# The recurrence stage of a two-layer kernel: its 512-token batches written out, layernorm two batches ahead, the dots of two heads issued as a pair

## What is computed

```python
xn = _layernorm(x)                       # (8, 512, 256), eps 1e-5
gamma = sigmoid(decay)                   # one per head, 4 heads of 64
v = (xn @ W_write.T) split in 4 heads
rk = xn split in 4 heads;  wk = rk moved one token later, zero first
# scan over chunks of 64 tokens; written without chunks, for token p of a head:
reads[p] = sum over k < p of gamma**(p-1-k) * (rk[p] . wk[k]) * v[k]
s = xn + (exp(log_alpha) * reads) @ W_read.T
```

## Time and profile before

| what | value |
|---|---|
| runs shown (3) | median 3754.51 us, 3751.19 to 3755.1 |
| the profiled execution, own time | 3755.62 us |
| its span, first to last instruction | 3753.9 us |
| granted TensorE clock, mean over the span | 0.947 |
| PE, PEld, DVE, ACT, POOL busy over the span | 91%, 69%, 66%, 58%, 31% |
| first dot and last `finish` of the recurrence | 2252.05 and 2529.12 us |

### The profile page before, as it was taken

How to read it: one execution, slowest core, us unless ns; L and a number is a source line. 1 busy time by engine, 2 the same in 40 slices (tenths; PEclk the granted TensorE clock), 3 DMA queues, 4 the chain that set the end, 5 groups by cost and what they waited for, 6 DMA issues and landing times. The chain is left out here.

```text
span 3753.9 us, 68147 instructions
## 1 busy us (share of the span) xinstructions
PE 3413.5 (91%) x19130; PEld 2589.2 (69%) x19130; DVE 2466.6 (66%) x7055; ACT 2174.9 (58%) x5066; POOL 1178.1 (31%) x1802
## 2 busy tenths in 40 slices
PE   2999999999999999989999978887999976799995
PEld 2777777777777777758888854444666655688885
DVE  5777777777777777776666643335666645466665
ACT  1777777777777777755565541113656551455553
POOL 1333333333333333334333420004131301244342
PEclk9999999999999999999999987887999985899998
DMA  4221222222122122234334420101111113445455
GB/s 160 46 49 43 49 49 45 47 49 48 44 49 49 43 49 49 47 108 141 117 123 138 131 95 23 34 28 41 27 30 28 28 43 135 150 120 141 129 133 151
DMA packets 177637, 282.42 MB, mean 75 GB/s; under 512 B 32499, under 2 KB 119283, under 8 KB 177523
## 3 DMA queue, kind: packets, MB, share of 16 engines
q1 hardware_dynamic: 162930, 261.03, 24.0%
q0 software_dynamic: 14592, 19.93, 3.3%
HBM read 161.89 MB, written 41.16 MB: 54 GB/s over the span
## 5 line engine op out<-in xcount | busy, mean ns | idle before, releaser
L723 POOL TENSOR_SCALAR at_p<-at_p,at_recip 128x128 f32<-128x128 f32 (+3 forms) x1028 | 537.0, 535 | 979.5 <-DVE at_recip L862 979.5
L773 ACT ACTIVATE at_p<-at_p,at_nmax 128x128 f32<-128x128 f32 (+3 forms) x1030 | 575.6, 559 | 290.1 <-DVE at_nmax L856 286.8
L856 DVE CUSTOM_DVE_ANT_0 at_p<-at_s_ps,at_bias 128x128 f32<-128x128 f32 (+3 forms) x1030 | 493.6, 479 | 153.7 <-PE at_s_ps L971 153.7
L978 PE MATMUL at_t_ps<-ident,at_p 128*128 128x128 f32 x2560 | 459.7, 277 | 0.4 <-POOL at_p L723 0.4
L970 PE MATMUL at_s_ps<-at_k_twice,at_q 128*128 128x128 f32 (+3 forms) x1030 | 387.7, 377 | 8.0 <-DVE at_nmax L856 1.2
L1748 DVE CUSTOM_DVE_ANT_0 aa_a_ps<-aa_a_ps,aa_hidden 128x128 f32<-128x128 f32 (+3 forms) x512 | 247.4, 507 | 175.9 <-PE aa_a_ps L1912 172.7
L971 PE MATMUL at_s_ps<-at_k_twice,at_q 128*128 128x128 f32 (+3 forms) x1030 | 332.3, 323 | 0.0
L978 PEld LDWEIGHTS at_t_ps<-ident,at_p 128*128 128x128 f32 x2560 | 294.7, 140 | 46.3 <-DVE at_pT L869 30.0
L988 PE MATMUL at_o_ps<-at_pT,at_v 128*64 128x512 f32 (+3 forms) x2064 | 306.3, 439 | 0.0
L1648 ACT ACTIVATE aa_pT<-aa_b_ps 128x512 f32<-128x512 f32 (+1 forms) x384 | 196.6, 529 | 178.6 <-PE aa_b_ps L1930 175.7
L988 PEld LDWEIGHTS at_o_ps<-at_pT,at_v 128*64 128x64 f32 x2064 | 136.7, 136 | 175.8 <-issue 156.9
(11 more groups left out here) (316 smaller groups left out, 8611.9 us busy)
## 6 DMA issues: line engine op xcount, KB each, us to landing
at_k_twice<-at_k_parts SPq DMA_DIRECT2D x260, 256.0 KB, 3.3
nw_w_raw<-in_w_all_dram SPq DMA_DIRECT2D x52, 1024.0 KB, 7.4
w_raw<-in_w_dram SPq DMA_DIRECT2D x57, 768.0 KB
ln_x<-in_x_dram SPq DMA_DIRECT2D x10, 512.0 KB, 4.7
nw_xh<-xh_dram SPq DMA_DIRECT2D x10, 512.0 KB, 4.3
nw_xl<-xl_dram SPq DMA_DIRECT2D x10, 512.0 KB, 4.9
rc_x<-x_dram SPq DMA_DIRECT2D x10, 512.0 KB, 3.8
at_w_raw<-in_w_heads_dram SPq DMA_DIRECT2D x18, 256.0 KB, 3.4
```

The costliest lines, as they stand in the source:

```text
L723: pool.tensor_scalar(p, p, recip[:, u:u + 1], 1.0, ALU.mult, ALU.mult).then_inc(scaled, 1)
L773: act.activation(p_sb[:, u, 0:N], p_sb[:, u, 0:N], ACT.Exp, bias=nmax[:, u:u + 1], scale=-1.0, accum_out=total[:, u:u + 1]).then_inc(exped, 1)
L856: dve.tensor_tensor_reduce(out=p_sb[:, u, 0:N], in0=s_ps[u % 2][:, 0:N], in1=bias[:, u % 2, S - N:S], scale=1.0, scalar=BIG, op0=ALU.add, ...
L978: ins = pe.transpose(t_ps[u % 2][:, k * P:k * P + P], p_sb[:, u, k * P:k * P + P], ident[:])
```

## The change

Nothing outside `recurrence_phase` changes. Inside:

- The loops over pairs of batches (`Fori`) are written out for all 8 batches; the last two loads of `x_in`, which nobody read, are gone, and so are SP's waits for a finished store.
- `norm` writes `y` directly, without the copy; transposition and squares read `y`. It is cut in three, `weigh_spread`, `sum_spread` and `norm`, and done for batch n+2 while batch n is worked on, between the decays.
- The banks `xT_ps` are gone: `turn` writes its two halves into `n_ps`, which it shares with `values` and `mix`. The freed banks go to `d_ps`, now four: two pairs, of one bank for each of two heads.
- `dots(n, g, t)` issues the products of heads 2g and 2g+1 for the same t one behind the other, in rows 0 to 63 and 64 to 127 of the array and in different banks. `turn`, `reads`, `values` and `mix` are cut in pieces that stand between the pairs. `mix` of batch n comes in batch n+1.
- ACT takes the half-turns one by one, and does `rms` behind them.

```diff
@@ tensor
-            def dots(n, par, h):
-                row = slice(HD * (h % 2), HD * (h % 2) + HD)
-                for i in range(TT):
-                    pe.wait_ge(decayed, n * (RH * TT) + (h * TT + i + 1))
-                    pe.matmul(d_ps[i % 2][:, 0:WIDTHS[i]], yT[par][row, h // 2, P * i:P * i + P],
-                              yT[par][row, h // 2, 1 + P * i:1 + S], start=True, stop=True).then_inc(dotted, 1)
+            def dots(n, g, t):
+                number = pair_no(n, g, t)          # (n * KT + g) * TT + t
+                if number >= 2:
+                    pe.wait_ge(decayed, 2 * number - 2)
+                for h in range(2):
+                    rows = slice(HD * h, HD * h + HD)
+                    pe.matmul(d_ps[t % 2][h][:, 0:WIDTHS[t]], yT[n % 2][rows, g, P * t:P * t + P],
+                              yT[n % 2][rows, g, 1 + P * t:1 + S], start=True, stop=True).then_inc(dotted, 1)
+            def turn(n, k):
+                pe.wait_ge(normed, n * TT + TT)
+                if n == 1:
+                    pe.wait_ge(value_out, k + 1)
+                if n >= 2:
+                    pe.wait_ge(s_done, 2 * (n - 2) + k + 1)
+                for i in range(TT):
+                    ins = pe.transpose(n_ps[k][:, P * i:P * i + P], y[:, n * TT + i, P * k:P * k + P], ident[:])
+                ins.then_inc(turned, 1)
...
+            def mix(n, half):
+                pe.wait_ge(read_out, 2 * n + 2)
+                if n + 1 < B:
+                    pe.wait_ge(value_out, 2 * (n + 1) + half + 1)
...
+            for n in range(B):
+                more = n + 1 < B
+                dots(n, 0, 0)
+                if n > 0:
+                    mix(n - 1, 0)
+                dots(n, 0, 1)
+                if n > 0:
+                    mix(n - 1, 1)
+                dots(n, 0, 2)
+                if more:
+                    turn(n + 1, 0)
+                dots(n, 0, 3)
+                if more:
+                    turn(n + 1, 1)
+                dots(n, 1, 0)
+                reads(n, 0, 0)
+                reads(n, 0, 1)
+                dots(n, 1, 1)
+                reads(n, 0, 2)
+                reads(n, 0, 3)
+                dots(n, 1, 2)
+                if more:
+                    values(n + 1, 0)
+                dots(n, 1, 3)
+                if more:
+                    values(n + 1, 1)
+                for i in range(TT):
+                    reads(n, 1, i)
+            mix(B - 1, 0)
+            mix(B - 1, 1)
@@ vector
+            for n in range(B):
+                decay_pair(n, 0, 0)
+                if n > 0:
+                    finish(n - 1, 0)
+                decay_pair(n, 0, 1)
+                if n > 0:
+                    finish(n - 1, 1)
+                decay_pair(n, 0, 2)
+                decay_pair(n, 0, 3)
+                invert_rms(n)
+                if n + 2 < B:
+                    weigh_spread(n + 2)
+                decay_pair(n, 1, 0)
+                decay_pair(n, 1, 1)
+                if n + 2 < B:
+                    sum_spread(n + 2)
+                decay_pair(n, 1, 2)
+                decay_pair(n, 1, 3)
+                if n + 2 < B:
+                    norm(n + 2)
+            finish(B - 1, 0)
+            finish(B - 1, 1)
```

More of the change, by code:

```diff
@@ L1087, in recurrence_phase @@
         dve_chain = sem("rc_dve_chain")
+        cleared = sem("rc_cleared")
         stats_done = sem("rc_stats_done")
@@ L1155, in _, with roots, rms, take_turn @@
         def _(act):
+            def roots(n):
+                act.wait_ge(var_done, n * TT + TT)
+                act.activation(std[:, 0, :], mv[:, :, 1], ACT.Sqrt, bias=eps[:, 0:1]).then_inc(std_done, 1)
+            def rms(n):
+                act.wait_ge(normed, n * TT + TT)
+                for i in range(TT):
+                    act.activation(squares[:, i, :], y[:, n * TT + i, :], ACT.Square,
+                                   accum_out=sq_sum[:, i:i + 1]).then_inc(squared, 1)
+                act.wait_ge(squared, n * TT + TT)
+                if n > 0:
+                    act.wait_ge(r1_done, n)
+                act.activation(std[:, 1, :], sq_sum[:], ACT.Sqrt, scale=1.0 / D, bias=eps[:, 1:2]).then_inc(rms_done, 1)
+            def take_turn(n, k):
+                act.wait_ge(turned, KT * n + k + 1)
+                act.activation(yT[n % 2][:, k, 1:S + 1], n_ps[k][:], ACT.Copy).then_inc(turn_out, 1)
+            def take_values(n, half):
+                act.wait_ge(valued, 2 * n + half + 1)
+                act.activation(v[n % 2][:, 2 * half:2 * half + 2, :].rearrange("p i d -> p (i d)"), n_ps[half][:],
+                               ACT.Copy).then_inc(value_out, 1)
+            def take_read(n, g):
+                act.wait_ge(read, 2 * n + g + 1)
+                act.activation(readT[:, g, :], r_ps[g][:], ACT.Copy).then_inc(read_out, 1)
             act.wait_ge(w_loaded, 64)
@@ L1178, in take_turn @@
[L1178 to L1195, removed]
+            act.wait_ge(cleared, 1)
+            roots(0)
             take_turn(0, 0)
+            take_turn(0, 1)
+            roots(1)
+            rms(0)
             take_values(0, 0)
[L1198 to L1206, removed]
+            take_values(0, 1)
@@ new lines, in sum_spread, with norm @@
+            def sum_spread(n):
+                dve.wait_ge(stats_done, TT * n + TT)
+                for i in range(TT):
+                    dve.bn_aggr(mv[:, i, :], stats[:, i, :]).then_inc(var_done, 1)
+            def norm(n):
+                dve.wait_ge(std_done, n + 1)
+                dve.reciprocal(rstd[:], std[:, 0, :]).then_inc(rstd_done, 1)
+                dve.wait_ge(rstd_done, n + 1)
+                for i in range(TT):
+                    dve.tensor_scalar(y[:, n * TT + i, :], x_in[n % 2][:, i, :], mv[:, i, 0:1], rstd[:, i:i + 1],
+                                      ALU.subtract, ALU.mult).then_inc(normed, 1)
@@ L1212, in _, with finish @@
+            def finish(n, half):
+                dve.wait_ge(mixed, 2 * n + half + 1)
+                if n >= 2 and half == 0:
+                    dve.wait_ge(s_stored[n % 2], 16 * (n // 2))
+                dve.tensor_tensor(s_sb[n % 2][:, 2 * half:2 * half + 2, :].rearrange("p i d -> p (i d)"), n_ps[half][:],
+                                  y[:, n * TT + 2 * half:n * TT + 2 * half + 2, :].rearrange("p i d -> p (i d)"), ALU.add)\
+                    .then_inc(s_done, 1)
             dve.memset(eps[:, 0:1], EPS_LN)
@@ L1221, in _ @@
             dve.tensor_scalar(gam[:], gam[:], -1.0, None, ALU.mult).then_inc(dve_chain, 1)
[L1223 to L1256, removed]
@@ L1258, in _ @@
-            norm(0, 0, 0)
-            invert_rms(0)
-            dve.wait_ge(pool_chain, 1 + RH)
[L1261 to L1271, removed]
+            weigh_spread(0)
@@ L1312, in mix @@
-            def mix(n):
-                pe.wait_ge(read_out, n * 2 + 2)
-                for half in range(2):
-                    for i in range(2):
-                        for g in range(KT):
-                            at = (2 * half + i) * P
-                            ins = pe.matmul(n_ps[half][:, i * D:i * D + D], readT[:, g, at:at + P], wr[:, g, :],
-                                            start=(g == 0), stop=(g == KT - 1))
-                    ins.then_inc(mixed, 1)
-            pe.wait_ge(w_loaded, 64)
@@ L1323, in _ @@
-            turn(0, 0)
-            values(0, 0)
-            with pe.Fori(0, B // 2) as pair:
-                for par in range(2):
-                    b, nxt = pair * 2 + par, 1 - par
-                    dots(b, par, 0)
-                    dots(b, par, 1)
-                    turn(b + 1, nxt)
-                    dots(b, par, 2)
-                    pe.wait_ge(value_out, b * 2 + 2)
-                    reads(b, par, 0)
-                    values(b + 1, nxt)
-                    dots(b, par, 3)
-                    reads(b, par, 1)
-                    pe.wait_ge(value_out, b * 2 + 4)
-                    mix(b)
+                if n == 1:
+                    pe.wait_ge(value_out, k + 1)
@@ new lines, in turn, with values @@
+                if n >= 2:
+                    pe.wait_ge(s_done, 2 * (n - 2) + k + 1)
+                for i in range(TT):
+                    ins = pe.transpose(n_ps[k][:, P * i:P * i + P], y[:, n * TT + i, P * k:P * k + P], ident[:])
+                ins.then_inc(turned, 1)
+            def values(n, half):
+                pe.wait_ge(turn_out, KT * n + KT)
+                for i in range(2):
+                    for k in range(KT):
+                        at = 1 + (2 * half + i) * P
+                        ins = pe.matmul(n_ps[half][:, i * D:i * D + D], yT[n % 2][:, k, at:at + P], ww[:, k, :],
+                                        start=(k == 0), stop=(k == KT - 1))
+                ins.then_inc(valued, 1)
@@ new lines, in mix @@
+            def mix(n, half):
+                pe.wait_ge(read_out, 2 * n + 2)
+                if n + 1 < B:
```

(25 more changed lines are left out.)

116 lines of the change are left out of this document (58 added, 58 removed).

## The result

The changed kernel takes 3632.36 us (median of 4 runs, 3630.57 to 3634.39), the kernel before 3754.81 us beside it (4 runs, 3751.19 to 3758.88): a ratio of 0.9674, 95% interval 0.9657 to 0.9691. Measured again later, beside another set of runs of the kernel before, the changed kernel took 3630.19 us (5 runs), ratio 0.9667, 0.9654 to 0.9681.

The account below looks back on a forecast made before the run. PE was taken to bound the stage: 157.6 us against 277.1, 119.5 less, 4 given back for the clock, so 3755.6 - 115.5 = 3640.1, said as 3640 us. Range 3625 to 3685 us, chance 0.8.

Parts of the forecast that it names:

- What bounds the stage, and the price of PE's work: Recurrence stage: PE is what the others wait for; its passes and switches cost 19.8 us a batch at full clock.
- Dots as pairs: Dots of two heads side by side in the array's rows: full overlap, 4.3 us a batch instead of 8.6.
- The bound of no overlap: Dots of a pair don't overlap at all: 8.6 us of dots, a batch of 24.1, 3674 us; chance 0.14.
- The rival of three steps a pair: Dots overlap in part, second head joining the first head's second pass: 6.45 us of dots, 3657 us; chance 0.12.
- Switches: Changes between kinds of product on PE: 17 a batch at 0.20 us, 3.4 us against 1.6 before.
- Waits: PE's waits for DVE's decays and finish in a full batch: none binds.
- the layout: One batch laid out from its first pair at 0, full clock, with the end times of PE's and DVE's pieces.
- the two smallest margins: PE's slack before waiting for DVE, at the second turn and at pair 4: 0.8 us.
- Clock: PE's clock in the stage: 1.0 over batches 1 to 7, with a half clock over part of batch 0.
- The 4 us given back for batch 0: Allowance of 4 us for a half clock over part of batch 0, which starts out of a stretch at 0.5.
- The sum, by its terms: Stage time: batch 0 16.8, batches 1 to 6 118.8, batch 7 16.5, ending 5.5; together 157.6 us against 277.1.
- two waits of 0.9 us: Batch 7, without turn and values: two waits of about 0.9 us between pairs that now touch.

Follow-up runs that it names:

- the kernel with 9 switches: Changed kernel with its pieces put together two by two, so 9 switches between kinds of product a batch in place of 17: 3618.17 us.
- A DVE block of 4 us: Changed kernel with the three layernorm pieces of batch n+2 in one block behind the decays of pair 3: 3634.77 us.
- the short layernorm: Kernel before, with layernorm statistics and scaling done on 16 of 256 features: 3751.88 us.
- the banks: Kernel before in its own order, turn writing into n_ps and a head's dots given four banks: 3719.77 us.
- the filling: Kernel before, with four unused 512-wide products put on PE between the second and third dot of head 1, where it waits: 3722.4 us.

## Why the prediction held

**What bounds the stage, and the price of PE's work.** Right. The 19.8 us a batch were the sum of PE's passes and switches alone, and 19.55 were measured, with PE busy in all of them.

**Dots as pairs.** Right, 1.06 us for the first pair. The bound of no overlap (3674 in the prediction, 34 us more) was built and took 32 us more. The rival of three steps a pair is out: the first passes of both heads start together, which the strict program order of the Trainium skill's page "TensorE: Matmul & The Clock Gate" ("What overlaps and what doesn't") would not give if a head's two passes follow one another in that order. In what order they are issued no view shows.

**Switches.** Right: 0.20 from one row, 0.19 over eight of them. The Trainium skill's rule that a change of tiling mode drains the array ("TensorEngine Tiling (Array Packing)", Key Properties) speaks against this order, the trace agrees, and the kernel with 9 switches is faster: by 14 us in the medians, 12 by the ratios to before, 10.4 in the stage itself (143.35 against 153.7 us).

**Waits.** Right that none binds in batches 1 to 6. Of the layout's ends, those checked agree within 0.6 us, and the two smallest margins, 0.8 us each in the layout, were 0.85 and 0.73. The margin at pair 6, 1.4 us in the layout, was 1.8. A DVE block of 4 us, which uses it up, costs 0.6 us a batch, and not the 3.84 that the prediction feared if PE's cover went.

**Clock.** Right in the middle, where it is 1.0. The 4 us given back for batch 0 were wrong: the clock rose before the first dots, at 2253.3, and stayed. The trace of before had shown this, too: its first dots, from 2252.05 on, lie in a stretch at 1.0.

```profile
2250.60:2257.30 6.70, 5.98 (x19) 2.90 (x18) 3.52 (x12) 0.84 (x3) 0.00 (x0) 1.00 0.00 0
```

**The sum, by its terms.** Batch 0 16.4 us (16.8 forecast); batches 1 to 6 117.3 (118.8); batch 7 to the last mix 15.6 (16.5 + 0.95); mix and addition 4.45 (4.6). Together 153.7 against 157.6 and the 4 of the clock: 7.9 us, which is the miss. The largest term beside the clock is batch 7. PE in batch 0 and in the second half of batch 7:

```profile
2254.47 1.77 PE L1320 MATMUL rc_d_ps<-rc_yT 64*128 64x512 f32 x8
2257.04 0.70 PE L1320 MATMUL rc_d_ps<-rc_yT 64*128 64x256 f32 x4 [0.80 <-DVE rc_prod L1239]
...
2393.89 0.93 PE L1320 MATMUL rc_d_ps<-rc_yT 64*128 64x256 f32 x8
2395.44 1.13 PE L1320 MATMUL rc_d_ps<-rc_yT 64*128 64x512 f32 x4 [0.62 <-DVE rc_prod L1239]
```

Of the two waits of 0.9 us that the prediction gave to batch 7, one came, of 0.62, at pair 4; pairs 6 and 7 touch without one. And pairs that touch have no switch between them, which the prediction left out: batch 7 has 10 switches where its sum has 13, and batch 0 has 13 where it has 15. Without the read's copy batch 7 takes 14.6 us. That this equals the 14.7 of PE's work in the prediction is chance: three switches less, 0.6 us, against the one wait.

**Where 123 us came from.** The stage lost 123.4. Idle time of PE fell from 277.2 - 233.1 = 44 us to 2.9: 41. The eight stretches at half clock took 116 us, but PE was idle in 22 of them, and that time is counted already. Its 93.8 us of work there would have taken half as long at full clock: 47. The sum over the eight:

```profile
sum 116.05, PE 93.76 PEld 50.82 DVE 46.66 ACT 25.63 POOL 0.00; mean PE 11.72 PEld 6.35 DVE 5.83 ACT 3.20 POOL 0.00
```

The overlap gives 32.6, and nine more switches a batch take about 14 back. 41 + 47 + 33 - 14 = 107. The other 16 us are in none of these terms. A part of them, as an estimate, is that PE counts as busy while the last pass before a wait runs out: a batch of before has 28.76 us of busy PE, less 5.5 for the half clock, 23.3, where the prediction prices its work at 22.3, so 8 us over eight batches. What the rest is, is not shown. These are shares of a sum, not what each part would give alone: the short layernorm gave 3 us of the stage and nothing that the runs can tell, the banks 33 us, the filling 31.

**What stays open.** What makes the clock fall in the old order. It fell with the gap, and with the gap filled after 4.5 us of nothing but single-head dots with short waits. It held with single-head dots between other products, and with pairs that wait 0.73 and 0.23 us. Either the long run of single-head dots by itself or the waits in it would fit; no kernel here separates the two.

## What to carry to other kernels

Two products that use one half of the array's rows each cost as much as one when they are issued together into banks of their own (1.06 us against 1.91); ask of every half-array product whether its partner can stand beside it. Where PE waits for small vector work, put full products between, but in groups: two pairs in line needed no more cover than one, four did, and each change of shape costs 0.2 us. Price a gap on PE together with the clock behind it: in the old order a gap 1.5 us shorter gave 0.3 us a batch, and useless products in the gap gave 31 us in all.

## What the hardware showed that was not expected

The clock fell to 0.5 with PE busy for 4.15 of the 4.5 us before (gap filled), so a PE without a long gap is no guarantee. And it took back most of a shorter wait: 3.84 to 2.35 us of gap, 34.57 to 34.25 us a batch in the mean. The batches of that kernel took 33.1 to 35.5 us though their instructions are the same; the three long ones are those in which the clock fell twice.
